# Expert stages of a four-layer network: second Gelu half also split into high and low f32r parts, its low part on GpSimd

## The chip, the cores and the metric

The kernel runs on one core of a Trainium2 chip. The metric is the device time of one execution in microseconds (us). The kernel before takes 1255.42 us, the median of 3 runs (1253.06 to 1261.09).

## The reference

The input x is [8, 512, 128] in float32. Four layers follow, each added to x: an RWKV-like time mixing, a mixture of experts, a causal attention with a phase term, and the same mixture of experts again. The change touches only the two expert layers. With the layer norm of x, written `tokens`, they compute:

```python
logits = tokens @ router_w.T
topv, topi = jax.lax.top_k(logits, K)              # K = 2 of E = 8 experts
w = jax.nn.softmax(topv, axis=-1)
gate = jnp.zeros((T, n_experts)).at[jnp.arange(T)[:, None], topi].add(w)
for e in range(n_experts):
    h = jax.nn.gelu(tokens @ w1[e].T, approximate=False)   # w1[e]: 256 x 128
    y = h @ w2[e].T                                        # w2[e]: 128 x 256
    out = out + gate[:, e:e + 1] * y
```

Every expert is computed for all tokens, and the gate (0 where an expert isn't chosen) weighs it.

## The kernel before

The program is a row of stages: time mixing (`rwkv_phase`), experts (`moe_phase`, tiles named moe_), attention, experts again (the same `moe_phase`), and the store. All instructions of a stage are written out engine by engine, and the order in each engine's stream is the order of the code. Engines meet only through semaphores.

In `moe_phase` the tokens are taken in 8 batches b of 512 tokens (T), channels on the 128 partitions. One step g = 8 b + e handles one expert e of one batch. The 256 hidden channels are two halves of 128 (k = 0, 1; HC = 2), so a step has

- `up(g)` on TensorE (L1774 on): for each half three matmuls in f32r into `ps_h`, weights high times x high, weights high times x low, weights low times x high (L1784 to L1786). A float32 value is split into a rounded high part and the rest, its low part; three f32r products stand for one float32 product.
- `gelu(g)` on ScalarE (L1859 on): of the first half a float32 Gelu into `hidden` (L1864) and the same Gelu rounded to f32r in `hidden_high` (L1865); of the second half the float32 Gelu alone (L1867). It waits for `down` of step g-2, because `hidden` has two places.
- `low_hidden(g)` on VectorE (L2012, L2017): `hidden_low` = `hidden` - `hidden_high` for the first half. Both inputs lie in SBUF.
- `down(g)` on TensorE (L1788 on): one float32 matmul for the second half (L1796, which the trace records as two instructions), then three f32r matmuls for the first half (L1800 to L1802), all into `ps_y`.
- `weigh(g)` on VectorE (L1986): `ps_y` (in PSUM) times the gate (in SBUF), and `accumulate(g)` (L1995): added to `total`, both inputs in SBUF. The first four steps of a stage are first copied out of PSUM by ScalarE (`keep_y`, L1878), and are weighed from SBUF.

TensorE's loop runs up(g+2), down(g). VectorE's loop runs in step g: low_hidden(g), weigh(g-1), accumulate(g-2), and then what is due. The table `WHEN` says in which step of which earlier batch the work that prepares batch c is done; for c of 4 and more: at e = 0 of batch c-2 the statistics of the norm (L199 to L208), at e = 1 the scaling (L218), at e = 2 the transposes on TensorE (`turn`, L1757), at e = 3 the copies (L1844, L1847) and the low part of x (L1925), at e = 4 the router (L1765), then five parts of the gates on VectorE at e = 5, 6, 7 and at e = 0, 1 of the next batch (L1934 to L1971), at e = 2 `fold` (L1770, waits for the last part of the gates). At e = 5 the output of the batch before is transposed (L1810), and at e = 6 added to x (`add`, L2000). So batches 1 to 5 carry statistics and scaling for a later batch in their steps 0 and 1, batch 0 carries two sets, and batches 6 and 7 none.

GpSimd has in this stage only eight small instructions, the power -0.5 of the variances (L224). It waits for the statistics, and the scaling waits for it.

At the start of the stage ScalarE rounds the up weights (w1) in four pieces and the down weights (w2), of the first halves only, in two (L1870, L1874); VectorE makes the low parts (L2005, L2010), some of them in the steps 0 and 1. `copies(0)` comes before them on ScalarE, and `gelu(0)`, `halve_gap(0)` (L1851, the tanh for which gates part 3 waits) behind.

## Time and profile before

| | |
|---|---|
| median of 3 runs | 1255.42 us |
| profiled execution, device time | 1258.44 us |
| its span, first to last instruction | 1256.7 us |
| TensorE busy | 1094.3 us (87%) |
| VectorE busy | 913.6 us (73%) |
| ScalarE busy | 658.0 us (52%) |
| GpSimd busy | 269.2 us (21%) |
| granted TensorE clock, mean | 0.918 of full |

The profile is one execution; busy times overlap between engines. The expert stages lie at about 300 to 523 us and 1025 to 1248 us of the span. A line's duration is from start to end of an instruction; where instructions of one engine follow without a gap, their starts are closer together than their durations, since the end of one overlaps the start of the next. "Idle before" is the time in which an engine had nothing, with what released it.

### The profile page before, as it was taken

The numbers are of one execution on the slowest core, as the hardware profiler recorded it, in microseconds if no ns is written. First come the engines' busy times: TensorE is split into PE (matmuls) and PEld (weight loads), VectorE is DVE, ScalarE is ACT, GpSimd is POOL, SyncE is SP. The second block draws the span as 40 slices with busy tenths as digits, with TensorE's granted clock in tenths as the row PEclk, the third lists the DMA queues.
The fourth block names the chain that finished last, engine by engine and source line by source line (L and its number), as shares of the span: only waits on it lengthen the run. The fifth ranks groups of instructions, "written<-read, shape, count | busy, mean of one in ns | idle before, by whom it ended". The sixth has DMA issues, their size and how long they took to land. (4 is left out here: it accounts for less than half of the span.)

```text
span 1256.7 us, 16161 instructions
## 1 busy us (share of the span) xinstructions
PE 1094.3 (87%) x5200; PEld 654.1 (52%) x5200; DVE 913.6 (73%) x1927; ACT 658.0 (52%) x1204; POOL 269.2 (21%) x300
## 2 busy tenths in 40 slices
PE   3888898975999999786888988989999969999996
PEld 1223333333666767444455555555656636767674
DVE  2778988993887776675766776767777628877775
ACT  1244434434555555388466665755755546555453
POOL 1455555650000000130122121222222210000000
PEclk9788888986999999888688988988989989999999
DMA  5000000000323322237977877778676212323221
GB/s 195 0 1 1 0 0 0 1 1 0 113 91 101 103 68 68 48 137 195 307 187 175 198 174 188 188 175 202 145 178 132 56 68 72 131 69 113 90 68 67
DMA packets 46478, 129.04 MB, mean 103 GB/s; under 512 B 6848, under 2 KB 8896, under 8 KB 39744
## 3 DMA queue, kind: packets, MB, share of 16 engines
q1 hardware_dynamic: 44352, 127.53, 37.1%
q8 instruction: 41, 0.67, 0.2%
q10 hardware_dynamic: 2048, 0.53, 0.2%
q14 instruction: 37, 0.30, 0.1%
HBM read 88.72 MB, written 36.70 MB: 100 GB/s over the span
## 5 line engine op out<-in xcount | busy, mean ns | idle before, releaser
L1483 DVE TENSOR_REDUCE attn_maxima<-attn_ps_p 128x1 f32<-128x512 f32 (+3 forms) x235 | 147.1, 638 | 81.3 <-PE attn_ps_p L987 56.8
L1864 ACT ACTIVATE moe_hidden<-moe_ps_h 128x512 f32<-128x512 f32 x128 | 76.3, 596 | 145.9 <-PE moe_ps_y L1802 144.1
L1402 POOL TENSOR_SCALAR_AFFINE_SELECT attn_probs<-attn_probs 128x512 f32<-128x512 f32 x128 | 83.8, 690 | 299.4 <-ACT attn_probs L1231 299.4
L982 PE MATMUL attn_ps_p<-attn_stack 96*128 96x384 f32 (+3 forms) x341 | 122.1, 401 | 7.8 <-DVE attn_maxima L1483 7.6
L1986 DVE TENSOR_TENSOR moe_gated<-moe_ps_y,moe_gate_all 128x512 f32<-128x512 f32 x106 | 73.2, 690 | 75.1 <-issue 46.7
L1030 PE MATMUL attn_ps_q<-attn_stack 128*128 128x128 f32 (+3 forms) x343 | 108.5, 380 | 18.2 <-DMA attn_stack<-attn_neg_max 14.5
L1784 PE MATMUL moe_ps_h<-moe_x_high,moe_w_high 128*128 128x512 f32 x256 | 107.3, 419 | 0.0
L1786 PE MATMUL moe_ps_h<-moe_x_high,moe_w_low 128*128 128x512 f32 x256 | 102.8, 402 | 0.0
L1785 PE MATMUL moe_ps_h<-moe_x_low,moe_w_high 128*128 128x512 f32 x256 | 102.3, 400 | 0.0
L1483 DVE TENSOR_REDUCE attn_maxima<-attn_ps_t 128x1 f32<-128x384 f32 (+3 forms) x117 | 74.6, 637 | 37.9 <-PE attn_ps_t L987 29.7
L1800 PE MATMUL moe_ps_y<-moe_hidden_high,moe_w_low 128*128 128x512 f32 x128 | 101.0, 789 | 0.0
L587 POOL TENSOR_TENSOR rwkv_rs<-rwkv_recept,rwkv_state 128x512 f32<-128x512 f32 x64 | 75.9, 1187 | 109.2 <-DVE rwkv_state L668 109.2
L668 DVE TENSOR_TENSOR_SCAN rwkv_state<-rwkv_decay,rwkv_kv 128x512 f32<-128x512 f32 x64 | 91.5, 1430 | 3.2
L2017 DVE TENSOR_TENSOR moe_hidden_low<-moe_hidden,moe_hidden_high 128x512 fp32r<-128x512 f32 x128 | 87.7, 685 | 6.2 <-ACT moe_hidden_high L1865 6.2
L1055 PE MATMUL attn_ps_o<-attn_probs,attn_v_ones 128*32 128x512 f32 (+3 forms) x1024 | 86.2, 456 | 1.7 <-POOL attn_probs L1402 1.7
L1030 PEld LDWEIGHTS attn_ps_q<-attn_stack 128*128 128x128 f32 x343 | 61.5, 202 | 42.3 <-DMA attn_stack<-attn_neg_max 16.9
L224 POOL TENSOR_TENSOR moe_rstd<-moe_var_eps,minus_half 128x4 f32<-128x4 f32 x16 | 16.1, 1008 | 311.4 <-DVE moe_var_eps L208 311.4
L982 PEld LDWEIGHTS attn_ps_p<-attn_stack 96*128 96x128 f32 x341 | 68.8, 215 | 20.3 <-DVE attn_maxima L1483 13.3
L1867 ACT ACTIVATE moe_hidden<-moe_ps_h 128x512 f32<-128x512 f32 x128 | 77.1, 602 | 0.4 <-PE moe_ps_h L1786 0.4
L1995 DVE TENSOR_TENSOR moe_total<-moe_total,moe_gated 128x512 f32<-128x512 f32 x112 | 76.4, 682 | 0.3
L1865 ACT ACTIVATE moe_hidden_high<-moe_ps_h 128x512 fp32r<-128x512 f32 x128 | 75.7, 591 | 0.0
L1228 ACT ACTIVATE attn_probs<-attn_ps_q 128x512 f32<-128x512 f32 x86 | 51.9, 603 | 36.6 <-PE attn_ps_q L1030 34.5
(256 smaller groups left out, 2441.5 us busy)
## 6 DMA issues: line engine op xcount, KB each, us to landing
moe_gate_all<-moe_gates SPq DMA_DIRECT2D x128, 256.0 KB, 4.8
attn_kept<-attn_parts SPq DMA_DIRECT2D x32, 768.0 KB, 4.7
attn_stack<-attn_kept SPq DMA_DIRECT2D x64, 384.0 KB
attn_stack<-attn_kept SPq DMA_DIRECT2D x64, 192.0 KB
attn_value<-attn_values SPq DMA_DIRECT2D x5, 1024.0 KB, 5.8
attn_value<-attn_values SPq DMA_DIRECT2D x5, 768.0 KB, 8.4
attn_values<-attn_early SPq DMA_DIRECT2D x2, 1792.0 KB, 5.7
attn_values<-attn_probs SPq DMA_DIRECT2D x2, 1792.0 KB, 21.7
```

What stands on the lines that cost most here:

```text
L668: nc.vector.tensor_tensor_scan(state[:, n, 1:T + 1], decay[:, s, :], kv[:, n % 2, :], 0.0, ALU.mult, ALU.add).then_inc(state_ready, 1)
L982: return mm(tiles(m)[:, i, :], stack[0][q][0:ROWS, h + i, t * P:(t + 1) * P], stack[1][q][0:ROWS, h + i, 0:(t + 1) * P], **flags)
L1030: return mm(ps_h[n % 3][:, at:at + width], stack[1][q][:, h, j * P:(j + 1) * P], stack[0][q][:, h, j * P:T], start=True, stop=True)
L1055: last = mm(ps_o[32 * hh:32 * hh + 32, j * P:T], v_ones[:, b % 2, j, 4 * g + hh, :], probs[:, g % 2, hh, at:at + width], start=(g % 2 == 0 ...
L1402: nc.gpsimd.affine_select(out=tile, in_=tile, compare_op=ALU.is_ge, fill=0.0, base=0, pattern=[[0, 4], [1, P]], channel_multiplier=-1).the ...
L1483: nc.vector.tensor_reduce(maxima[:, u % 2, h:h + heads, t], tiles, AX_X, ALU.max).then_inc(g_free, 1)
L1784: mm(out[:], w1_high[:, cols], x_high[:, c % 3, :], start=True, stop=False)
L1785: mm(out[:], w1_high[:, cols], x_low[:, c % 3, :], start=False, stop=False)
L1786: mm(out[:], w1_low[:, cols], x_high[:, c % 3, :], start=False, stop=True).then_inc(up_done, 1)
L1800: mm(ps_y[s][:], w2_low[:, first], hidden_high[:, s, :], start=False, stop=False)
L1867: fn(hidden[:, s, T:], ps_h[s][1][:], ACT.Gelu).then_inc(gelu_done, 1)
L2017: tt(hidden_low[:, s, :], hidden[:, s, 0:T], hidden_high[:, s, :].bitcast(F32), ALU.subtract).then_inc(low_ready, 1)
```

## The change

The second Gelu half is treated as the first. ScalarE computes it twice, in float32 and rounded to f32r (one more instruction a step, L1868 of the new file). Its low part is computed by GpSimd (`second_low`, L1911), which waits for the step's Gelu. `down` has six f32r matmuls in place of one float32 and three f32r; the first half comes first now, and its wait for `low_hidden` with it. The down weights are rounded and split for both halves, in four pieces of 512 columns in place of two, interleaved with the up weights. Nothing else changes; the order of the due work stays.

```diff
-        hidden_high = sb("hidden_high", [P, 2, T], F32R)
-        hidden_low = sb("hidden_low", [P, 2, T], F32R)
-        w2_high = sb("w2_high", [P, NE * C], F32R)
-        w2_low = sb("w2_low", [P, NE * C], F32R)
+        hidden_high = sb("hidden_high", [P, 2, HT], F32R)
+        hidden_low = sb("hidden_low", [P, 2, HT], F32R)
+        w2_high = sb("w2_high", [P, NE * HC * C], F32R)
+        w2_low = sb("w2_low", [P, NE * HC * C], F32R)
...
-        W1_STEP, W2_STEP = (1, 3, 4, 5), (2, 6)
+        W1_STEP, W2_STEP = (1, 3, 5, 7), (2, 4, 6, 8)
...
+                if g < NE and e % 2 == 0:
+                    pe.wait_ge(split, W2_STEP[e // 2])
+                pe.wait_ge(low_ready, g + 1)
+                mm(ps_y[s][:], w2_low[:, first], hidden_high[:, s, 0:T], start=True, stop=False)
+                mm(ps_y[s][:], w2_high[:, first], hidden_high[:, s, 0:T], start=False, stop=False)
+                mm(ps_y[s][:], w2_high[:, first], hidden_low[:, s, 0:T], start=False, stop=False)
                 pe.wait_ge(gelu_done, g * HC + 2)
-                mm(ps_y[s][:], w2_cols[:, second], hidden[:, s, T:], start=True, stop=False)
-                pe.wait_ge(low_ready, g + 1)
-                if g in (0, NE // 2):
-                    pe.wait_ge(split, W2_STEP[g // (NE // 2)])
-                mm(ps_y[s][:], w2_low[:, first], hidden_high[:, s, :], start=False, stop=False)
-                mm(ps_y[s][:], w2_high[:, first], hidden_high[:, s, :], start=False, stop=False)
-                mm(ps_y[s][:], w2_high[:, first], hidden_low[:, s, :], start=False, stop=True).then_inc(down_done, 1)
+                mm(ps_y[s][:], w2_low[:, second], hidden_high[:, s, T:], start=False, stop=False)
+                mm(ps_y[s][:], w2_high[:, second], hidden_high[:, s, T:], start=False, stop=False)
+                pe.wait_ge(second_low_ready, g + 1)
+                mm(ps_y[s][:], w2_high[:, second], hidden_low[:, s, T:], start=False, stop=True).then_inc(down_done, 1)
...
-                fn(hidden[:, s, T:], ps_h[s][1][:], ACT.Gelu).then_inc(gelu_done, 1)
+                fn(hidden[:, s, T:], ps_h[s][1][:], ACT.Gelu)
+                fn(hidden_high[:, s, T:], ps_h[s][1][:], ACT.Gelu).then_inc(gelu_done, 1)
...
+            def second_low(g):
+                s = g % 2
+                pool.wait_ge(gelu_done, (g + 1) * HC)
+                if g >= 2:
+                    pool.wait_ge(down_done, g - 1)
+                nc.gpsimd.tensor_tensor(hidden_low[:, s, T:], hidden[:, s, T:], hidden_high[:, s, T:].bitcast(F32),
+                                        ALU.subtract).then_inc(second_low_ready, 1)
+
             norm.on_pool(pool, 0)
             for b in range(NB):
                 for e in range(NE):
+                    second_low(b * NE + e)
                     for c in due("stats", b, e):
                         norm.on_pool(pool, c)
...
                     low_hidden(g)
-                    if g == 0:
-                        split_w1(2)
-                    if g == 1:
-                        split_w1(3)
-                        split_w2(1)
+                    if g < 3:
+                        split_w2(g + 1)
+                    if g < 2:
+                        split_w1(g + 2)
```

On TensorE, in step 0 of the first batch, from the last matmul of an `up` on, the stream before has one float32 matmul (L1796) and three f32r ones after `fold`:

```order
L1786 MATMUL moe_ps_h<-moe_x_high,moe_w_low 128x512
L1770 MATMUL moe_ps_r<-identity,moe_gate 32x128
L1796 MATMUL moe_ps_y<-moe_hidden,experts_in_w 128x512
L1800 MATMUL moe_ps_y<-moe_hidden_high,moe_w_low 128x512
L1801 MATMUL moe_ps_y<-moe_hidden_high,moe_w_high 128x512
L1802 MATMUL moe_ps_y<-moe_hidden_low,moe_w_high 128x512
```

and of the change, at the same place:

```order
L1783 MATMUL moe_ps_h<-moe_x_high,moe_w_low 128x512
L1767 MATMUL moe_ps_r<-identity,moe_gate 32x128
L1795 MATMUL moe_ps_y<-moe_hidden_high,moe_w_low 128x512
L1796 MATMUL moe_ps_y<-moe_hidden_high,moe_w_high 128x512
L1797 MATMUL moe_ps_y<-moe_hidden_low,moe_w_high 128x512
L1799 MATMUL moe_ps_y<-moe_hidden_high,moe_w_low 128x512
L1800 MATMUL moe_ps_y<-moe_hidden_high,moe_w_high 128x512
L1802 MATMUL moe_ps_y<-moe_hidden_low,moe_w_high 128x512
```

The float32 matmul has gone, three f32r matmuls of the second half stand behind those of the first; `hidden_low` of the first half is read by the third.

On GpSimd, in the first expert stage, the difference of the two streams is this (a minus is before, a plus is the change):

```order
-L224 TENSOR_TENSOR moe_rstd<-moe_var_eps,minus_half 128x4 x8
+L1904 UNCONDITIONAL_BRANCH
+L224 TENSOR_TENSOR moe_rstd<-moe_var_eps,minus_half 128x4
+L1911 TENSOR_TENSOR moe_hidden_low<-moe_hidden,moe_hidden_high 128x512
+L224 TENSOR_TENSOR moe_rstd<-moe_var_eps,minus_half 128x4
+L1911 TENSOR_TENSOR moe_hidden_low<-moe_hidden,moe_hidden_high 128x512
+L224 TENSOR_TENSOR moe_rstd<-moe_var_eps,minus_half 128x4
+L1911 TENSOR_TENSOR moe_hidden_low<-moe_hidden,moe_hidden_high 128x512 x7
+L224 TENSOR_TENSOR moe_rstd<-moe_var_eps,minus_half 128x4
+L1911 TENSOR_TENSOR moe_hidden_low<-moe_hidden,moe_hidden_high 128x512 x8
```

The small powers were alone; now 64 subtractions of 128x512 stand between them, one a step, and the power of a statistics step stands behind that step's own subtraction and ahead of the next one's.

On ScalarE, at the start of the first expert stage, before, from the rounding of x on:

```order
L1847 CAST moe_x_high<-moe_ps_t 128x512
L1870 CAST moe_w_high<-experts_in_w 128x512
L1874 CAST moe_w_high<-experts_in_w 128x512
L1870 CAST moe_w_high<-experts_in_w 128x512 x3
L1874 CAST moe_w_high<-experts_in_w 128x512
L1864 ACTIVATE moe_hidden<-moe_ps_h 128x512
L1865 ACTIVATE moe_hidden_high<-moe_ps_h 128x512
L1867 ACTIVATE moe_hidden<-moe_ps_h 128x512
L1851 ACTIVATE moe_tanh_gap<-moe_gap_of_two 128x4
```

and of the change, from the fifth rounding of weights on:

```order
L1871 CAST moe_w_high<-experts_in_w 128x512
L1874 CAST moe_w_high<-experts_in_w 128x512
L1871 CAST moe_w_high<-experts_in_w 128x512
L1874 CAST moe_w_high<-experts_in_w 128x512
L1864 ACTIVATE moe_hidden<-moe_ps_h 128x512
L1865 ACTIVATE moe_hidden_high<-moe_ps_h 128x512
L1867 ACTIVATE moe_hidden<-moe_ps_h 128x512
L1868 ACTIVATE moe_hidden_high<-moe_ps_h 128x512
L1851 ACTIVATE moe_tanh_gap<-moe_gap_of_two 128x4
```

There are eight roundings where there were six, and four Gelus where there were three, ahead of the tanh.

## Rows read from the trace of the kernel before

**Rows 1.** Busy time by engine in both expert stages, and in steps 1-7 of batch 0

```profile
core 0: us, PE busy (x) PEld busy (x) DVE busy (x) ACT busy (x) POOL busy (x), PEclk, DMA share, GB/s
300.00:523.50 223.50, 210.04 (x840) 148.15 (x840) 169.91 (x462) 117.40 (x235) 8.07 (x8) 0.97 0.24 77
1025.00:1256.70 231.70, 209.94 (x840) 148.09 (x840) 170.20 (x463) 117.61 (x235) 8.07 (x8) 0.96 0.27 92
317.60:340.60 23.00, 22.89 (x98) 16.59 (x98) 20.03 (x58) 15.13 (x32) 1.01 (x1) 1.00 0.28 93
```

**Rows 2.** Timeline of TensorE and ScalarE, one quiet step (start, duration, ... [idle before])

```profile
506.51 0.40 PE L1784 MATMUL moe_ps_h<-moe_x_high,moe_w_high 128*128 128x512 f32 x1
506.71 0.60 ACT L1864 ACTIVATE moe_hidden<-moe_ps_h 128x512 f32<-128x512 f32 x1 [1.37 <-PE moe_ps_y L1802]
...
507.21 0.59 ACT L1865 ACTIVATE moe_hidden_high<-moe_ps_h 128x512 fp32r<-128x512 f32 x1
...
507.69 0.60 ACT L1867 ACTIVATE moe_hidden<-moe_ps_h 128x512 f32<-128x512 f32 x1
...
507.92 1.02 PE L1796 MATMUL moe_ps_y<-moe_hidden,experts_in_w 128*128 128x512 f32 x2
...
509.00 0.39 PE L1801 MATMUL moe_ps_y<-moe_hidden_high,moe_w_high 128*128 128x512 f32 x1
...
509.23 0.40 PE L1802 MATMUL moe_ps_y<-moe_hidden_low,moe_w_high 128*128 128x512 f32 x1
...
509.46 0.39 PE L1784 MATMUL moe_ps_h<-moe_x_high,moe_w_high 128*128 128x512 f32 x1
```

**Rows 3.** Durations by line (min/median/max ns), GpSimd and VectorE, time mixing and expert stage

```profile
L587 POOL TENSOR_TENSOR rwkv_rs<-rwkv_recept,rwkv_state x64: 1087/1259/1452, 42.0 to 281.4; 128x512 f32<-128x512 f32 x64
L203 DVE TENSOR_TENSOR rwkv_sums<-rwkv_stats x8: 171/946/1054, 10.9 to 220.7; 128x12 f32<-128x12 f32 x8
L203 DVE TENSOR_TENSOR moe_sums<-moe_stats x16: 171/172/173, 300.7 to 1175.9; 128x12 f32<-128x12 f32 x16
L651 DVE SCALAR_TENSOR_TENSOR rwkv_z<-rwkv_z,rwkv_gate x8: 665/1516/1610, 100.1 to 296.0; 128x512 f32<-128x512 f32 x8
L662 DVE TENSOR_TENSOR rwkv_kv<-rwkv_key,rwkv_ps_v x64: 654/677/689, 40.0 to 279.2; 128x512 f32<-128x512 f32 x64
```

**Rows 4.** Timeline of GpSimd and VectorE in the time mixing

```profile
91.94 1.08 POOL L581 TENSOR_TENSOR rwkv_xf<-rwkv_mixed,rwkv_xT 128x512 f32<-128x512 f32 x1
92.00 1.05 DVE L203 TENSOR_TENSOR rwkv_sums<-rwkv_stats 128x12 f32<-128x12 f32 x1
```

**Rows 5.** Timeline of VectorE and GpSimd, step 6 of batch 2 to step 2 of batch 3

```profile
388.85 0.69 DVE L1986 TENSOR_TENSOR moe_gated<-moe_ps_y,moe_gate_all 128x512 f32<-128x512 f32 x1 [0.95 <-PE moe_ps_y L1802]
...
390.61 0.68 DVE L2000 TENSOR_TENSOR x_rows<-x_rows,moe_ps_t 128x512 f32<-128x512 f32 x1
391.20 0.68 DVE L2017 TENSOR_TENSOR moe_hidden_low<-moe_hidden,moe_hidden_high 128x512 fp32r<-128x512 f32 x1
...
393.63 0.68 DVE L2017 TENSOR_TENSOR moe_hidden_low<-moe_hidden,moe_hidden_high 128x512 fp32r<-128x512 f32 x1
...
394.75 0.69 DVE L1986 TENSOR_TENSOR moe_gated<-moe_ps_y,moe_gate_all 128x512 f32<-128x512 f32 x1 [0.44 <-issue]
...
397.73 1.01 POOL L224 TENSOR_TENSOR moe_rstd<-moe_var_eps,minus_half 128x4 f32<-128x4 f32 x1 [25.33 <-DVE moe_var_eps L208]
...
398.03 0.68 DVE L2017 TENSOR_TENSOR moe_hidden_low<-moe_hidden,moe_hidden_high 128x512 fp32r<-128x512 f32 x1
...
399.83 1.11 DVE L218 TENSOR_SCALAR moe_xn<-x_rows,moe_mean,moe_rstd 128x128 f32<-128x128 f32 x4
...
401.00 0.66 PE L1757 MATMUL moe_ps_t<-identity,moe_xn 128*128 128x128 f32 x4 [0.44 <-DVE moe_xn L218]
...
401.41 0.21 DVE L1971 TENSOR_TENSOR moe_gate<-moe_first,moe_second 128x32 f32<-128x32 f32 x1
```

**Rows 6.** Timeline of the start of the first expert stage

```profile
308.55 0.62 ACT L1874 CAST moe_w_high<-experts_in_w 128x512 fp32r<-128x512 f32 x1
...
309.58 0.60 ACT L1864 ACTIVATE moe_hidden<-moe_ps_h 128x512 f32<-128x512 f32 x1 [0.40 <-PE moe_ps_h L1786]
...
311.58 0.17 DVE L1960 TENSOR_SCALAR moe_share<-moe_tanh_gap 128x4 f32<-128x4 f32 x1 [0.50 <-ACT moe_tanh_gap L1851]
...
317.71 0.66 PE L1757 MATMUL moe_ps_t<-identity,moe_xn 128*128 128x128 f32 x4 [1.69 <-DVE moe_xn L218]
```

**Rows 7.** Timeline of the end of the first expert stage

```profile
516.01 0.60 ACT L1864 ACTIVATE moe_hidden<-moe_ps_h 128x512 f32<-128x512 f32 x1 [1.81 <-PE moe_ps_y L1802]
...
517.87 0.68 DVE L2017 TENSOR_TENSOR moe_hidden_low<-moe_hidden,moe_hidden_high 128x512 fp32r<-128x512 f32 x1
...
519.18 0.40 PE L1802 MATMUL moe_ps_y<-moe_hidden_low,moe_w_high 128*128 128x512 f32 x1
```

28 lines of the change are left out of this document (11 added, 17 removed).

## The prediction

> **What bounds the kernel now.** I first read the busy time of the two expert stages, the only code touched: TensorE is busy 210.04 of 223.5 us and 209.94 of 231.7, VectorE 170, ScalarE 117, GpSimd 8 [rows 1]. So TensorE paces them. Then one quiet step in the timelines [rows 2]. From the first matmul of one `up` (506.51) to that of the next (509.46) a step takes 2.95 us with no gap: `up` 1.41 (six f32r matmuls of 0.235), `down` 1.54. In `down` an f32r matmul costs 0.23 from start to start (509.00, 509.23, 509.46), so the float32 one costs 1.54 - 3 x 0.23 = 0.85. ScalarE idles 1.37 us ahead of its three Gelus, so a fourth seems free. Last, the places where TensorE doesn't pace. In steps 0 and 1 of batches 1 to 5 VectorE has statistics, gates and scaling on top of its share; there the transposes at 401.00 come after 0.44 us of idle, "until" the scaling, and from the `weigh` at 394.75 to the last gate operation (start 401.41) VectorE has no idle time [rows 5]. At the start of the stage the transposes wait 1.69 us for the scaling [rows 6].
>
> **Removed and added, on TensorE.** Each of 128 steps trades 0.85 for 3 x 0.233 = 0.70: 0.15 saved, 19.2 us in all if nothing else changed. A quiet step falls to 2.80. The Trainium skill, "TensorE: Matmul & The Clock Gate", section "Wait — 56ns, not 53.3ns?", gives 215.7 ns from start to start for 512 columns at full clock. An estimate by it would be 0.85 - 0.65 = 0.20 a step, so 6.4 us more gained; the trace shows 0.23, at a granted clock of 1.00, and decides.
>
> **Added on ScalarE.** One more Gelu, 0.48 from start to start. Four end 2.05 us after the first starts (0.50 + 0.48 + 0.48 + 0.59 [rows 2]); with idle 1.37 in a step of 2.95, that leaves about 0.74 in one of 2.80. I cost it at nothing; without that cover it would be 0.48 a step. Only the start of the stage pays, below.
>
> **Added on GpSimd, and what it does to VectorE.** 128 subtractions of 128x512. The nearest row is its own multiply of that shape, 1.09 us at least, median 1.26 [rows 3]. I take 1.05 to 1.1. It fits in GpSimd's idle time. But the trace of the time mixing shows what happens beside it. VectorE's L203, twelve elements wide, takes 0.17 us in the expert stages, yet up to 1.05 and 0.95 in the median in the time mixing [rows 3]; in the timeline it starts at 92.00 and lasts 1.05 while GpSimd's L581 runs from 91.94 for 1.08 [rows 4]. L651, both inputs in SBUF, has a median of 1.52 against 0.67 at best; L662, one input in PSUM, never passes 0.69 in 64 executions [rows 3]. So a VectorE instruction with two SBUF inputs waits until GpSimd's ends, and one that reads PSUM doesn't. In the expert stages nothing met GpSimd so far. Now `low_hidden`, `accumulate`, most of the gates and the small statistics can meet it; `weigh`, `add`, the low part of x don't.
>
> In a quiet step the subtraction fits: it runs from 2.1 to 3.2 us after the Gelu's release, `weigh` starts at 2.8 and the `accumulate` behind it at 3.4. Where VectorE is behind, it doesn't. I walk a statistics batch from the `weigh` at 388.85 (call it 0) [rows 5]:
>
> Before: `add` at 1.76, `low_hidden` of step 7 at 2.35, that of the next step 0 at 4.78, `weigh` at 5.90 after 0.44 idle, `low_hidden` of step 1 at 9.18, scaling at 10.98, gates done 12.8. `fold` on TensorE waits for those.
>
> After: step 7's Gelus start with the `weigh`, so its subtraction runs 2.05 to 3.15; `low_hidden` waits 0.8, until 3.15. `weigh`, `accumulate` (0.6 each) to 4.95. The next subtraction takes over at 4.95, until 6.0: the gates part 2 wait 1.05. They take 0.6, `low_hidden` of step 0 ends at 7.2; TensorE would have reached its `down` at 6.8, starts at 7.25. `weigh`, `accumulate` to 8.4, statistics 1.6 to 10.0, gates part 3 to 10.5, `low_hidden` to 11.1, where TensorE wanted it at 10.05. GpSimd's power runs 10.05 to 11.05 and the subtraction behind it 11.1 to 12.15: `weigh` passes, `accumulate` waits 0.45 and ends at 12.75, scaling 13.8, gates 14.5. That is 1.7 us later than before. The four steps left until the next such `weigh` are paced by TensorE: -0.6. **Sum +1.1 a batch, five batches: +5.5 a stage.**
>
> **Batch 0.** Before the first Gelu there are two more roundings, 0.52 each, of which 0.40 was idle, and the start goes from 309.58 to 310.1; the fourth Gelu puts the tanh, and gates part 3, from 311.58 to 312.35 [rows 6]. The first subtraction then holds gates part 4 until 313.3, one more split costs 0.6 ahead of the statistics, and the transposes go from 317.71 to 319.6: +1.9. Up to 340.6 VectorE gets two more splits (1.2) and five waits for GpSimd that a walk like the one above gives (1.0, 0.85, 0.6, 0.85, 0.45); it had 23.00 - 20.03 = 2.97 us idle there [rows 1]. 1.9 + 4.95 - 2.97 = **+3.9**.
>
> **Batches 6 and 7 and the end.** Batch 6 has no statistics: 8 x -0.15, and 0.85 of the same two early waits: -0.35. Batch 7: -1.2. At the end the last Gelus start at 516.01, done 518.06; `low_hidden`, from 517.87, holds GpSimd until 518.55, its subtraction ends at 519.6, and the last matmul starts then, in place of 519.18 [rows 7]: with the last step's saving lost, +0.5.
>
> **Sum.** 3.9 + 5.5 - 0.35 - 1.2 + 0.5 = 8.35 a stage, 16.7 for both. The second stage I take as the first. From the profiled execution's 1258.4 that is 1275.1; it stands 3.0 above the median of the runs shown, so for the median I forecast 1255.4 + 16.7 = 1272.
>
> **The rivals.**
>
> *No such waits matter, and the kernel gets faster.* GpSimd and VectorE may meet less than in my walk, since each meeting hangs on a few tenths (the first: subtraction from 2.05, `low_hidden` at 2.35). With no meeting, a statistics batch gains the 0.44 idle's part and its quiet steps, 2 x 0.15 + 4 x 0.15 = 0.9; a stage is then -0.1 (batch 0: extra splits and tanh +1.1, steps -1.2), -4.5, -2.4, +0.3: -6.7, twice -13.4, 1242. It speaks for it that ScalarE and GpSimd have room; against it that in batch 0 and around steps 7, 0, 1 VectorE goes without a break, so a subtraction must push something. It decides when a batch's waits on its unbroken chain come to less than about 0.6 us in place of 2.3. Chance 0.2.
>
> *Half of the waits.* Some fall under `weigh`, `add` or the statistics' first part. With 1.2 us of waits a batch in place of 2.3, stages come out near 0: 1250 to 1266. Chance 0.25.
>
> *The walk holds.* Own range 1266 to 1280, chance 0.43.
>
> *The scaling is held too.* L218 reads one SBUF tensor and writes SBUF. No row shows it beside a big GpSimd instruction. If it is held as well, scaling beside a subtraction loses up to 1.05 us in each of seven preparations a stage: 14.7 us for both, 1272 + 15 = 1287. The Trainium skill, "SBUF — State Buffer", section "Who interferes with whom", says that a tensor_scalar can enter a mode that takes both read ports, and then whoever issues second blocks fully; by that rule L218 belongs here. Chance 0.12.
>
> **How the numbers follow.** About 1% is what a measurement of this kernel can tell from no change: 1243 and 1268 are its edges. Faster: the first rival about at its edge and a little more, 0.17. Slower: most of the walk (0.38), the held scaling (0.12) and a small part of the half case (0.05): 0.55. Between: 0.28. The range reaches from the upper part of the first rival, 1245, to the held scaling, 1288; what is left out is about 0.1 on each side.
>
> **What would show it.** TensorE: a quiet step of 2.80, and six matmuls in `down` at 0.23. VectorE: `low_hidden` and `accumulate` with maxima near 1.7 where they had 0.69, L1986 unchanged; idle time of TensorE ahead of the first matmul of `down`, released by `low_hidden`, in steps 0 and 1, and ahead of the transposes above 1 us. If L218 stays at 0.34, the last rival is out. If `low_hidden` and `accumulate` keep 0.68, my theory is wrong, and so it is if GpSimd's subtraction takes 2 us: then TensorE waits for GpSimd itself. If the saving is not 0.15 a step, that term is wrong.

## The result, and the profile after

The changed kernel takes 1303.17 us (median of 4 runs, 1302.65 to 1303.64); the kernel before takes 1258.26 us beside it (1253.06 to 1262.67). The ratio is 1.0354, with an interval of 1.0321 to 1.0387: slower, and by 45 us where 17 were forecast. The time lies above the forecast range of 1245 to 1288.

The page of the profile after, span and busy times:

```profile
span 1301.0 us, 16803 instructions
PE 1093.1 (84%) x5328; PEld 684.8 (53%) x5328; DVE 972.3 (75%) x1931; ACT 721.4 (55%) x1336; POOL 444.2 (34%) x428
```

The two expert stages, as in [rows 1] (same columns: TensorE, weight loads, VectorE, ScalarE, GpSimd, granted clock):

```profile
294.60:540.40 245.80, 210.68 (x904) 162.71 (x904) 199.51 (x464) 148.97 (x301) 95.89 (x72) 0.94 0.21 70
1043.20:1301.00 257.80, 213.36 (x904) 165.29 (x904) 199.47 (x464) 149.09 (x301) 96.66 (x72) 0.92 0.24 83
```

In the first stage TensorE is still busy 210.68 us, as before (210.04), but the stage takes 245.8 us instead of 223.5, so TensorE is not busy for 35 us of it instead of 13. VectorE's busy time rose from 169.9 to 199.5 us with as many instructions (464 and 462): some of them take longer. GpSimd works 96 us where it worked 8.

From the first transposes of the stage to the start of attention, the first stage grew from 219.8 us to 242.0 (303.84 to 523.64, now 298.49 to 540.45). From its first transposes to the store, the second grew from 220.5 (1029.44 to 1249.96) to 247.2 (1047.14 to 1294.38). That is 48.9 us more in the stages, 22.2 in the first and 26.7 in the second, of which 4.6 came back in code that wasn't touched: the time mixing ends 5.4 earlier, attention takes 0.9 more, the end 0.1 less. In the time mixing TensorE was granted 0.90 of its full clock in the first 290 us where it was 0.88 in the execution before; I read that as a difference between executions.

**The quiet step** came out as forecast. Timeline of TensorE and ScalarE, to compare with [rows 2]:

```profile
503.06 0.60 ACT L1864 ACTIVATE moe_hidden<-moe_ps_h 128x512 f32<-128x512 f32 x1 [0.72 <-PE moe_ps_y L1802]
...
504.27 0.40 PE L1795 MATMUL moe_ps_y<-moe_hidden_high,moe_w_low 128*128 128x512 f32 x1
504.51 0.40 PE L1796 MATMUL moe_ps_y<-moe_hidden_high,moe_w_high 128*128 128x512 f32 x1
...
505.21 1.29 POOL L1911 TENSOR_TENSOR moe_hidden_low<-moe_hidden,moe_hidden_high 128x512 fp32r<-128x512 f32 x1 [1.49 <-ACT moe_hidden_high L1868]
505.43 0.39 PE L1802 MATMUL moe_ps_y<-moe_hidden_low,moe_w_high 128*128 128x512 f32 x1
...
505.86 0.60 ACT L1864 ACTIVATE moe_hidden<-moe_ps_h 128x512 f32<-128x512 f32 x1 [0.73 <-PE moe_ps_y L1802]
```

From Gelu to Gelu it is 2.80 us (503.06 to 505.86), matmuls in `down` start every 0.23, and ScalarE idles 0.72 (0.74 forecast). Each part of TensorE's gain is there. The last matmul at 505.43 starts when the subtraction of 505.21 has just begun; the one it reads is that of the step before, 502.42 to 503.72.

**The rest** of a batch is not. Timeline of VectorE, GpSimd, one Gelu and the waits of TensorE, from step 7 of batch 2 to step 2 of batch 3, to compare with [rows 5]:

```profile
396.78 1.29 POOL L1911 TENSOR_TENSOR moe_hidden_low<-moe_hidden,moe_hidden_high 128x512 fp32r<-128x512 f32 x1 [1.72 <-ACT moe_hidden_high L1868]
397.05 1.57 DVE L2024 TENSOR_TENSOR moe_hidden_low<-moe_hidden,moe_hidden_high 128x512 fp32r<-128x512 f32 x1
...
399.58 1.39 POOL L1911 TENSOR_TENSOR moe_hidden_low<-moe_hidden,moe_hidden_high 128x512 fp32r<-128x512 f32 x1 [1.51 <-ACT moe_hidden_high L1868]
399.75 1.28 DVE L1955 SCALAR_TENSOR_TENSOR moe_rest<-moe_first,moe_logits 128x32 f32<-128x32 f32 x1
...
405.03 1.01 POOL L224 TENSOR_TENSOR moe_rstd<-moe_var_eps,minus_half 128x4 f32<-128x4 f32 x1 [4.06 <-DVE moe_var_eps L208]
...
405.40 0.62 ACT L1868 ACTIVATE moe_hidden_high<-moe_ps_h 128x512 fp32r<-128x512 f32 x1
...
406.01 2.95 POOL L1911 TENSOR_TENSOR moe_hidden_low<-moe_hidden,moe_hidden_high 128x512 fp32r<-128x512 f32 x2
...
406.16 0.47 PE L1795 MATMUL moe_ps_y<-moe_hidden_high,moe_w_low 128*128 128x512 f32 x1 [0.84 <-DVE moe_hidden_low L2024]
406.53 1.31 DVE L2002 TENSOR_TENSOR moe_total<-moe_total,moe_gated 128x512 f32<-128x512 f32 x1
...
407.76 2.05 DVE L218 TENSOR_SCALAR moe_xn<-x_rows,moe_mean,moe_rstd 128x128 f32<-128x128 f32 x4
...
409.87 0.66 PE L1754 MATMUL moe_ps_t<-identity,moe_xn 128*128 128x128 f32 x4 [2.02 <-DVE moe_xn L218]
```

Call it a meeting when a VectorE instruction runs beside one of GpSimd and lasts longer for it. The three meetings of the walk are there: `low_hidden` 1.57 instead of 0.68, the first operation of the gates part 2 1.28 instead of 0.19, `accumulate` 1.31 instead of 0.68. There is a fourth: the row of GpSimd at 406.01 holds two subtractions, the one of step 1 and right behind it the one of step 2. Step 1's had to wait behind the power (405.03, until 406.04), and by then step 2's Gelus were done too (405.40, until 406.02). Beside the second subtraction the four scalings take 2.05 instead of 1.11. Of the 14 preparations behind the first of each stage, 11 have a scaling of 2.04 to 2.06; the other three keep 1.1. The transposes then come after 2.02 us of idle instead of 0.44. Starts of the transposes in the first stage were 348.49, 374.82, 401.00, 427.34, 453.70 before, a period of 26.2 to 26.4; now they are 350.79, 379.73, 409.87, 438.61, 468.80, so a batch takes 28.7 to 28.9 or 30.1 to 30.2.

Durations by line over the whole execution (min/median/max ns), for [rows 3]:

```profile
L1911 POOL TENSOR_TENSOR moe_hidden_low<-moe_hidden,moe_hidden_high x128: 1260/1296/1857, 306.9 to 1288.4; 128x512 fp32r<-128x512 f32 x128
L2024 DVE TENSOR_TENSOR moe_hidden_low<-moe_hidden,moe_hidden_high x128: 676/684/1576, 309.0 to 1288.2; 128x512 fp32r<-128x512 f32 x128
L2002 DVE TENSOR_TENSOR moe_total<-moe_total,moe_gated x112: 672/681/1681, 328.8 to 1292.0; 128x512 f32<-128x512 f32 x112
L1993 DVE TENSOR_TENSOR moe_gated<-moe_ps_y,moe_gate_all x106: 673/691/694, 333.2 to 1291.3; 128x512 f32<-128x512 f32 x106
L218 DVE TENSOR_SCALAR moe_xn<-x_rows,moe_mean,moe_rstd x64: 331/335/1290, 297.3 to 1222.8; 128x128 f32<-128x128 f32 x64
```

Medians hide it: of these lines the maxima of `low_hidden`, `accumulate` and the scaling moved and the medians didn't. `weigh`, which reads PSUM, kept 694.

**The clock.** In two-microsecond windows behind three of the waits, with one at full clock for comparison (390 to 392; same columns as rows 1; the granted clock is the third number from the end):

```profile
380.00:382.00 2.00, 2.00 (x10) 1.35 (x9) 2.00 (x4) 1.08 (x2) 1.22 (x1) 0.78 0.00 0
382.00:384.00 2.00, 2.00 (x6) 1.61 (x6) 1.63 (x6) 0.00 (x0) 0.00 (x0) 0.50 0.00 0
...
390.00:392.00 2.00, 2.00 (x12) 1.64 (x12) 0.53 (x1) 0.59 (x2) 1.17 (x1) 1.00 0.90 279
...
440.00:442.00 2.00, 2.00 (x6) 1.56 (x5) 1.11 (x2) 2.00 (x5) 0.01 (x1) 0.50 0.07 16
...
470.00:472.00 2.00, 2.00 (x6) 1.51 (x6) 1.29 (x2) 2.00 (x6) 0.00 (x0) 0.50 0.05 12
```

Behind the waits at 379.73, 438.61 and 468.80 TensorE is granted 0.50 for two to four microseconds, the lower of its levels (1.2 instead of 2.4 GHz), and two microseconds hold 6 of its matmuls instead of 12. Behind the waits at 350.79 and 409.87 it isn't. In both stages, behind batch 0, 7 of 10 such waits are followed by a fall. The periods that contain a fall take 30.1 to 31.1 us, those that don't 28.7 to 28.9. Before, there was no such fall between 313 and 523 us. In batch 0 the change's clock also falls behind the wait of 4.25 us (0.57 at 316 to 318).

### The profile page after: what moved, and what is told of

It reads as the page before. It is cut to its first block and busy times, and to the rows that moved or that the text cites. A ratio compares the mean times of both kernels' runs of the same rounds, so it can differ in the third digit from the quotient of the medians.

```text
span 1301.0 us, 16803 instructions
## 1 busy us (share of the span) xinstructions
PE 1093.1 (84%) x5328; PEld 684.8 (53%) x5328; DVE 972.3 (75%) x1931; ACT 721.4 (55%) x1336; POOL 444.2 (34%) x428
## 5 line engine op out<-in xcount | busy, mean ns | idle before, releaser
L1911 POOL TENSOR_TENSOR moe_hidden_low<-moe_hidden,moe_hidden_high 128x512 fp32r<-128x512 f32 x128 | 176.9, 1384 | 241.0 <-ACT moe_hidden_high L1868 241.0
L1781 PE MATMUL moe_ps_h<-moe_x_high,moe_w_high 128*128 128x512 f32 x256 | 110.4, 431 | 0.0
L1783 PE MATMUL moe_ps_h<-moe_x_high,moe_w_low 128*128 128x512 f32 x256 | 106.5, 416 | 0.0
L1782 PE MATMUL moe_ps_h<-moe_x_low,moe_w_high 128*128 128x512 f32 x256 | 106.1, 415 | 0.0
L2024 DVE TENSOR_TENSOR moe_hidden_low<-moe_hidden,moe_hidden_high 128x512 fp32r<-128x512 f32 x128 | 96.4, 753 | 4.8 <-ACT moe_hidden_high L1865 4.6
L2002 DVE TENSOR_TENSOR moe_total<-moe_total,moe_gated 128x512 f32<-128x512 f32 x112 | 88.0, 786 | 0.3
L1868 ACT ACTIVATE moe_hidden_high<-moe_ps_h 128x512 fp32r<-128x512 f32 x128 | 78.9, 617 | 0.0
L1865 ACT ACTIVATE moe_hidden_high<-moe_ps_h 128x512 fp32r<-128x512 f32 x128 | 75.9, 593 | 0.0
```

Of the source, the lines that this page charges most:

```text
L1781: mm(out[:], w1_high[:, cols], x_high[:, c % 3, :], start=True, stop=False)
L1782: mm(out[:], w1_high[:, cols], x_low[:, c % 3, :], start=False, stop=False)
L1783: mm(out[:], w1_low[:, cols], x_high[:, c % 3, :], start=False, stop=True).then_inc(up_done, 1)
L1911: nc.gpsimd.tensor_tensor(hidden_low[:, s, T:], hidden[:, s, T:], hidden_high[:, s, T:].bitcast(F32), ALU.subtract).then_inc(second_low_re ...
L2002: tt(total[:, b % 2, :], total[:, b % 2, :], gated[:, g % 3, :], ALU.add).then_inc(summed, 1)
L2024: tt(hidden_low[:, s, 0:T], hidden[:, s, 0:T], hidden_high[:, s, 0:T].bitcast(F32), ALU.subtract).then_inc(low_ready, 1)
```

## The experiments

Eleven kernels ran. Each was timed beside the kernel before on the same chip; that one had medians of 1257.31, 1258.00 and 1256.08 us in the three groups (x1 to x4; x5, x7 to x9; x10, x12, x13). Period and idle time are those of the fourth to the last transposes of the first stage. The last column adds up the two stages in the one profiled execution, each from its first transposes, to the start of attention and to the store; it leaves out the code that no kernel changes, in which the executions differ by several us (attention takes 501.5 to 511.7 us in these traces).

| kernel | median us | ratio to before (95%) | period of a batch, first stage | idle ahead of the transposes | both stages, us |
|---|---|---|---|---|---|
| before | 1256.08 to 1258.26 | 1 | 26.2 to 26.4 | 0.44 to 1.21 | 440.3 |
| changed | 1303.17 | 1.0354 (1.0321 to 1.0387) | 28.7 to 30.2 | 1.96 to 2.29 | 489.2 |
| x1 GpSimd only writes | 1246.09 | 0.9888 (0.9825 to 0.9951) | 25.2 to 25.5 | 0.54 to 1.17 | 436.0 |
| x2 half of the columns | 1261.15 | 1.0035 (1.0007 to 1.0062) | 26.4 to 26.6 | 0.92 to 1.15 | 446.7 |
| x3 before, plus a subtraction | 1310.73 | 1.0383 (1.0320 to 1.0445) | 30.6 to 31.0 | 1.66 to 3.09 | 497.7 |
| x4 filler matmuls | 1296.81 | 1.0313 (1.0253 to 1.0373) | 28.8 to 29.0 | 0.32 to 0.64 | 478.3 |
| x5 low part on VectorE | 1266.11 | 1.0063 (1.0034 to 1.0091) | 27.0 to 27.1 | 1.10 to 1.24 | 449.4 |
| x7 subtraction in steps 3 to 6 | 1258.60 | 1.0003 (0.9973 to 1.0032) | 25.2 to 25.4, first 27.2 | 0.51 to 1.54 | 446.1 |
| x8 in steps 7, 0, 1, 2 | 1289.58 | 1.0268 (1.0235 to 1.0300) | 27.0, then 28.5 to 30.3 | 1.75 to 2.02 | 476.5 |
| x10 all but step 2 | 1280.52 | 1.0169 (1.0130 to 1.0208) | 27.6 to 27.8, first 29.3 | 1.01 to 2.04 | 465.7 |
| x12 batch 0 only | 1256.44 | 0.9999 (0.9972 to 1.0026) | 25.2 to 25.5 | 0.52 to 1.54 | 445.8 |
| x9 mixed, steps 3 to 6 | 1249.98 | 0.9947 (0.9918 to 0.9976) | 25.5 to 25.7, first 26.3 | 0.44 to 0.60 | 431.6 |
| x13 mixed, steps 2 to 6 | 1256.19 | 1.0005 (0.9979 to 1.0031) | 26.3 to 26.5, first 27.3 | 0.34 to 1.55 | 439.5 |

**x1_write_only.** Is it the reading by GpSimd, or the extra work on TensorE and ScalarE?

```diff
-                nc.gpsimd.tensor_tensor(hidden_low[:, s, T:], hidden[:, s, T:], hidden_high[:, s, T:].bitcast(F32),
-                                        ALU.subtract).then_inc(second_low_ready, 1)
+                nc.gpsimd.memset(hidden_low[:, s, T:].bitcast(F32), 0.0).then_inc(second_low_ready, 1)
```

> The changed kernel, but GpSimd writes zeros into the low part of the second half (a memset of 128x512) in place of the subtraction, so the low part of the second half is left out; everything else (four Gelus, six f32r matmuls, four pieces of down weights, the wait for GpSimd) stays. Theory (a GpSimd instruction that reads SBUF holds up VectorE instructions with two SBUF inputs and the scaling, and the long waits let TensorE's clock fall): the holds go, the saving of 0.15 us a step stays, about 1245 us, VectorE lines back at 0.68. Rival one (what costs is the fourth Gelu, the extra splits or the new order in down): stays at about 1300. Rival two (any GpSimd instruction on SBUF holds VectorE, writing ones too): VectorE's two-input lines still reach over 1 us, 1265 to 1280.

It took 1246.09 us. Durations by line:

```profile
L1911 POOL MEMSET moe_hidden_low<- x128: 524/525/644, 308.8 to 1236.8; 128x512 f32 x128
L2023 DVE TENSOR_TENSOR moe_hidden_low<-moe_hidden,moe_hidden_high x128: 679/683/693, 310.1 to 1236.6; 128x512 fp32r<-128x512 f32 x128
L218 DVE TENSOR_SCALAR moe_xn<-x_rows,moe_mean,moe_rstd x64: 334/343/628, 299.3 to 1175.1; 128x128 f32<-128x128 f32 x64
```

So all of the change but the subtraction gains about 12 us by the medians, close to the 13.4 that the prediction gave for no meetings. In the trace the two stages gain only 4.3 (436.0 against 440.3): the periods are shorter by 0.9, but up to the fourth transposes the stages take 2.9 and 5.1 us more than before. The rest of the 12 lies in other code or in the spread of the four runs (1239 to 1251, the profiled one at 1251). A GpSimd instruction that only writes doesn't hold `low_hidden` (693 at most, though dozens of `low_hidden` and `accumulate` overlap a MEMSET). It does hold the scaling, up to 628.

**x2_half_columns.** Does the cost follow the length of the subtraction?

```diff
-                nc.gpsimd.tensor_tensor(hidden_low[:, s, T:], hidden[:, s, T:], hidden_high[:, s, T:].bitcast(F32),
-                                        ALU.subtract).then_inc(second_low_ready, 1)
+                half = T + T // 2
+                nc.gpsimd.tensor_tensor(hidden_low[:, s, T:half], hidden[:, s, T:half],
+                                        hidden_high[:, s, T:half].bitcast(F32), ALU.subtract).then_inc(second_low_ready, 1)
```

> The changed kernel, but GpSimd subtracts only 256 of the 512 columns (half of the low part of the second half isn't made, and the last matmul of down takes the first half's low part in its place). Theory: each hold shrinks from 1.3 us to about 0.75, the transposes wait less than 1.5 us, and the clock no longer falls in the middle of a stage: a batch with statistics takes 26.5 to 27.5 us in place of 28.7 to 30.2, about 1270 us in all. Rival (GpSimd's cost is the latency or the number of its instructions, not how long each holds the port): 1295 to 1303.

It took 1261.15 us. A subtraction of 256 columns takes 0.74 in the median in place of 1.30, `low_hidden` is at most 1.02 and the scaling at most 0.76. The period is 26.4 to 26.6, where 28.7 to 30.2 and 25.4 stand at both ends. Half the length costs a good quarter of the whole (1246 to 1261 of 1246 to 1303), less than the 1270 that I had put. The maxima show that each meeting is shorter; that there are also fewer of them is my reading.

**x3_before_plus_sub.** The kernel before with the subtraction alone, whose result nobody reads, and for which the last matmul of `down` waits:

```diff
+                pe.wait_ge(extra_done, g + 1)
...
+                nc.gpsimd.tensor_tensor(unused[:, s, :], hidden[:, s, T:], hidden_high[:, s, :].bitcast(F32),
+                                        ALU.subtract).then_inc(extra_done, 1)
```

> The kernel before, with one thing added: a GpSimd subtraction of 128x512 from hidden and hidden_high into a tile that nobody reads, once a step, with TensorE's last matmul of down waiting for it as in the change. TensorE, ScalarE and the splits are as before. Theory: the holds alone cost nearly the whole loss and the missing saving of 19 us comes on top of it only partly: VectorE's chain in steps 6 to 1 is as long as in the change, a batch with statistics takes 28.5 to 30 us, 1290 to 1305 us in all. Rival (the loss is in the rest of the change): 1258 to 1265.

It took 1310.73 us, 5.7 us above the expected range; that the order of TensorE's old `down` fits worse with the subtraction is my reading, which no run takes apart. Timeline in the first stage:

```profile
407.42 2.95 POOL L1915 TENSOR_TENSOR moe_unused<-moe_hidden,moe_hidden_high 128x512 fp32r<-128x512 f32 x2
...
408.75 0.49 PE L1804 MATMUL moe_ps_y<-moe_hidden_low,moe_w_high 128*128 128x512 f32 x1 [0.54 <-POOL moe_unused L1915]
409.17 2.05 DVE L218 TENSOR_SCALAR moe_xn<-x_rows,moe_mean,moe_rstd 128x128 f32<-128x128 f32 x4
...
411.27 0.76 PE L1758 MATMUL moe_ps_t<-identity,moe_xn 128*128 128x128 f32 x4 [2.02 <-DVE moe_xn L218]
```

Without any of the other parts the same pair of subtractions stands beside the same scaling, and the same wait of 2.02 follows. TensorE itself waits for GpSimd here, 0.54 in this place. x1 and x3 together show that the subtraction on GpSimd is the cause.

**x4_filler.** What does the clock cost? Fourteen short matmuls into the bank of the transposes stand ahead of each wait for the scaling, from the transposes of batch 1 on. They are extra work whose results the transposes overwrite.

```diff
-                pe.wait_ge(norm.normed, c + 1)
...
+                if c >= 1:
+                    for _ in range(14):
+                        mm(ps_t[:, 0:256], w1_high[:, 0:P], x_high[:, (c - 1) % 3, 0:256], start=True, stop=True)
+                pe.wait_ge(norm.normed, c + 1)
```

> The changed kernel, with 14 matmuls of 256 columns that nobody needs on TensorE ahead of each wait of the transposes for the scaling (from batch 1's on), written where the transposes write later. Theory that the falls of TensorE's clock to half are part of the loss, some 1.4 us each: they go in the middle of the stages, batches that took 30.1 us take 28.7, about 8 to 12 us less in all, 1291 to 1296. Rival (the clock isn't on the path, VectorE is, since the steps behind the transposes have slack): 1301 to 1305, or more where the filler itself is late.

It took 1296.81 us, 0.8 above its range. Windows at the place of a fall, and in batch 0:

```profile
382.00:384.00 2.00, 2.00 (x9) 1.60 (x10) 1.92 (x7) 0.23 (x2) 0.00 (x0) 1.00 0.00 0
...
316.00:318.00 2.00, 2.00 (x7) 1.62 (x6) 1.93 (x11) 2.00 (x5) 0.00 (x0) 0.59 0.83 218
```

From the fourth transposes on, the clock stays at full and each period is 28.8 to 29.0, with none of 30.1; in batch 0, where 2.60 us of idle are left, it still falls. That shows that the later falls come from the waits and make the difference between 28.8 and 30.1. By the medians they cost 6 us; the intervals of the two ratios (1.0313 and 1.0354) overlap, so the times alone don't fix the size. In the traces the two stages take 10.9 us less than those of the change, of which up to 1.6 is another wait, for the gates' transfer (see the next section).

**x5_on_vector.** The second low part on VectorE, right behind `low_hidden`; GpSimd doesn't subtract.

```diff
+            def second_low(g):
+                s = g % 2
+                v.wait_ge(gelu_done, (g + 1) * HC)
+                tt(hidden_low[:, s, T:], hidden[:, s, T:], hidden_high[:, s, T:].bitcast(F32),
+                   ALU.subtract).then_inc(second_low_ready, 1)
```

> The changed kernel with the second low part made by VectorE, right behind low_hidden of the same step; GpSimd has only its eight small powers a stage again, all else as changed. Theory (the meetings of a 1.3 us GpSimd instruction with VectorE are what costs): an operation of VectorE costs it 0.6 us from start to start, a meeting up to 1.3. Steps 7, 0 and 1 of a statistics batch get 3 x 0.6 = 1.8 us more on the unbroken chain, the four paced steps give 0.6 back: period 26.3 + 1.2 = 27.5, batch 0 two us more, end nothing: about 8 us a stage, 1258 + 16 = 1274, range 1262 to 1288. L218 stays at 0.34 and low_hidden at 0.68. Rival (it is the work itself, and not who does it or what it meets): like the change, 1297 to 1303, or more, since VectorE is the busier engine.

It took 1266.11 us, with 27.0 to 27.1 a batch (27.5 expected) and the scaling at 0.348 at most. The engine that was already late does all of the extra work, and the kernel is 37 us faster than with the work on the idle engine. So the place on an idle engine was worth less than nothing: a subtraction costs VectorE 0.6 us when it does it, and up to 1.1 more in one instruction (1.28 for 0.19) when GpSimd does.

**x7_quiet_steps and x8_busy_steps.** Where do the meetings cost? x7 subtracts in steps 3 to 6 of each batch and writes zeros in the others, x8 the reverse.

```diff
-                nc.gpsimd.tensor_tensor(hidden_low[:, s, T:], hidden[:, s, T:], hidden_high[:, s, T:].bitcast(F32),
-                                        ALU.subtract).then_inc(second_low_ready, 1)
+                if 3 <= g % NE <= 6:
+                    nc.gpsimd.tensor_tensor(hidden_low[:, s, T:], hidden[:, s, T:],
+                                            hidden_high[:, s, T:].bitcast(F32), ALU.subtract).then_inc(second_low_ready, 1)
+                else:
+                    nc.gpsimd.memset(hidden_low[:, s, T:].bitcast(F32), 0.0).then_inc(second_low_ready, 1)
```

> The changed kernel, in which GpSimd makes the low part of the second half only in steps 3 to 6 of each batch; in steps 0, 1, 2 and 7 it writes zeros to it (a memset of 0.52 us), so that the low part of the second half is left out of the result there. If the cost lies where VectorE has no slack (steps 7, 0, 1, 2), this one comes near the writing alone (1246): 1246 to 1253, turns every 25.2 to 25.6 us with idle under 1.2, clock at full. Rival, that each subtraction costs something wherever it stands: about half way between 1246 and 1303, 1270 to 1280.

> The other half: GpSimd subtracts only in steps 7, 0, 1 and 2, and writes zeros in steps 3 to 6, so that the low part of the second half is left out of the result there. If the cost lies in the steps without slack, it is the change's own: 1292 to 1303, turns every 28.5 us or more with idle of about 2 us, and the clock falls behind these waits. Rival, cost spread evenly: 1270 to 1280.

x8 took 1289.58 us, 2.4 below its range, but much nearer to the change than to the rival's 1270 to 1280, with turns after 2.02 us of idle and the clock at 0.50 at 402 to 404 and at 0.57 around 434. x7 took 1258.60 us, 5.6 above its range. Its turns (transposes), in the timeline of the first stage:

```profile
400.19 1.11 DVE L218 TENSOR_SCALAR moe_xn<-x_rows,moe_mean,moe_rstd 128x128 f32<-128x128 f32 x4
...
401.36 0.66 PE L1754 MATMUL moe_ps_t<-identity,moe_xn 128*128 128x128 f32 x4 [0.51 <-DVE moe_xn L218]
```

From the fifth transposes of the stage on (376.14) its periods are 25.2 to 25.4, the same as with no subtraction at all (x1): in the quiet steps it is free there. Of the 12.5 us that it takes more than x1, 9.9 lie ahead of that: from the first transposes to the fifth it takes 77.5 us in the first stage and 82.9 in the second, x1 takes 73.0 and 77.5. My division was too coarse: in batch 0, with two sets of statistics, the splits and the early steps weighed from SBUF, no step is quiet, and the turn behind it (27.2) is late as well.

**x12_batch_zero.** The subtraction in batch 0 alone, zeros behind.

```diff
-                if 3 <= g % NE <= 6:
+                if g < NE:
```

(the minus line is that of x7).

> The changed kernel with the subtraction in batch 0 alone and writes of zeros in batches 1 to 7 (the low part of the second half is left out of the result there). It prices the meetings of batch 0. From the starts of the transposes, the change takes 4.8 and 5.5 us more than the writing alone (1246) up to the first turn behind batch 0: 1246 + 10 = 1256, range 1252 to 1259, with periods of 25.2 to 25.4 behind. Rival, that batch 0 costs the 3.9 a stage of the prediction less the extra roundings and splits, which the writing alone has too (about 1 to 2): 1248 to 1250.

It took 1256.44 us, as expected: meetings in batch 0 cost 10 us in both stages by the medians, 14 by the ratios (0.9999 against 0.9888, each uncertain by 3 to 8 us). In the traces the two stages take 9.8 us more than x1's, and no more than x7's (445.8 and 446.1), which subtracts only in steps 3 to 6 of this batch. The start of the first stage shows two meetings of batch 0, one with a small TENSOR_SCALAR, for which no row of before shows a meeting. Timeline of the changed kernel, for [rows 6]:

```profile
306.90 1.29 POOL L1911 TENSOR_TENSOR moe_hidden_low<-moe_hidden,moe_hidden_high 128x512 fp32r<-128x512 f32 x1 [9.61 <-ACT moe_hidden_high L1868]
306.95 1.27 DVE L1967 TENSOR_SCALAR moe_share<-moe_tanh_gap 128x4 f32<-128x4 f32 x1 [1.22 <-ACT moe_tanh_gap L1851]
...
313.54 1.26 POOL L1911 TENSOR_TENSOR moe_hidden_low<-moe_hidden,moe_hidden_high 128x512 fp32r<-128x512 f32 x1
313.61 2.04 DVE L218 TENSOR_SCALAR moe_xn<-x_rows,moe_mean,moe_rstd 128x128 f32<-128x128 f32 x4 [1.12 <-POOL moe_rstd L224]
...
315.70 0.55 PE L1754 MATMUL moe_ps_t<-identity,moe_xn 128*128 128x128 f32 x3 [4.25 <-DVE moe_xn L218]
```

A TENSOR_SCALAR of four elements with one SBUF input takes 1.27 in place of 0.17, and the scaling is held here too; TensorE waits 4.25 where it waited 1.69.

**x10_not_step_two.** Is the fourth meeting, that of the scaling, caused by step 2's subtraction, and what is it worth? Zeros are written in step 2 alone.

```diff
-                if 3 <= g % NE <= 6:
+                if g % NE != 2:
```

(the minus line is again that of x7).

> The changed kernel, in which GpSimd writes zeros in place of the subtraction in step 2 of each batch alone (the low part of the second half is left out of the result there). In the trace of the change the last of the subtractions that stand beside the scaling L218 is that of step 2. If it holds the scaling and nothing else: L218 back to about 0.34, the turn's wait from 2.0 to about 1.1, the period from 28.8 to 27.9, and the clock stays full, since waits of 1.1 us did not bring it down in the kernel with the work on VectorE: 1303 - 9 - 6 = 1288, range 1282 to 1294. Rival, that the scaling would be late anyhow because of the meetings ahead of it: 1297 to 1303.

It took 1280.52 us, 1.5 us below the range. Timeline in the first stage:

```profile
406.93 1.29 POOL L1912 TENSOR_TENSOR moe_hidden_low<-moe_hidden,moe_hidden_high 128x512 fp32r<-128x512 f32 x1
...
407.46 1.31 DVE L2005 TENSOR_TENSOR moe_total<-moe_total,moe_gated 128x512 f32<-128x512 f32 x1
408.16 0.53 POOL L1915 MEMSET moe_hidden_low<- 128x512 f32 x1
...
408.69 1.10 DVE L218 TENSOR_SCALAR moe_xn<-x_rows,moe_mean,moe_rstd 128x128 f32<-128x128 f32 x4
...
409.86 0.66 PE L1754 MATMUL moe_ps_t<-identity,moe_xn 128*128 128x128 f32 x4 [1.08 <-DVE moe_xn L218]
```

`accumulate` is still held (1.31), the scaling is back at 1.10, the wait is 1.08, and behind batch 0 the clock fell only once in the stage, after the one wait of 2.04 at 352.92. The steady period of 27.6 to 27.8 is the walk of the prediction, which gave 26.3 + 1.1 = 27.4. In batch 0 nothing changed (the transposes still wait 4.26 us): there it is the subtraction of step 1 that stands beside the scaling.

**x9_hybrid.** Can the gain be had without the meetings? It starts from the kernel before and takes the new step only where VectorE has slack and no more due work of batch 0 lies; the down weights of the second halves are rounded and split in steps 4 to 6 of batch 1. ScalarE's fourth Gelu and GpSimd's subtraction go with these steps.

```diff
+        SPLIT = [g for g in range(2 * NE, NB * NE - 1) if 3 <= g % NE <= 6 or g >= 6 * NE + 2]
...
+                if g in SPLIT:
...
+                    mm(ps_y[s][:], w2_low[:, first], hidden_high[:, s, 0:T], start=True, stop=False)
+                    mm(ps_y[s][:], w2_high[:, first], hidden_high[:, s, 0:T], start=False, stop=False)
+                    mm(ps_y[s][:], w2_high[:, first], hidden_low[:, s, 0:T], start=False, stop=False)
+                    pe.wait_ge(gelu_done, g * HC + 2)
+                    mm(ps_y[s][:], second_w2_low[:, first], hidden_high[:, s, T:], start=False, stop=False)
+                    mm(ps_y[s][:], second_w2_high[:, first], hidden_high[:, s, T:], start=False, stop=False)
+                    pe.wait_ge(second_low_ready, SPLIT.index(g) + 1)
+                    mm(ps_y[s][:], second_w2_high[:, first], hidden_low[:, s, T:], start=False, stop=True).then_inc(down_done, 1)
+                    return
```

> The kernel before, with the new step (six f32r matmuls, four Gelus, subtraction on GpSimd) only in steps 3 to 6 of batches 2 to 5 and in the steps from step 2 of batch 6 on but the last: 29 steps a stage. Nothing is left out. If the saving of 0.15 us a step is real and the subtraction is free where VectorE has slack: 2 x 29 x 0.15 = 8.7 us less, about 1249, ratio 0.993. If the subtraction costs wherever it stands, or the extra roundings and VectorE's split of the down weights in steps 4 to 6 of batch 1 are not hidden: 1256 to 1262, ratio 1.000 to 1.004.

It took 1249.98 us, the forecast 1249: faster than before by 0.5% (0.2 to 0.8%), and than the change by 4%. The two stages take 8.7 us less in its trace (431.6 against 440.3), and 8.7 were expected. The scaling keeps 0.347 at most, and TensorE waits as before:

```profile
393.61 1.11 DVE L218 TENSOR_SCALAR moe_xn<-x_rows,moe_mean,moe_rstd 128x128 f32<-128x128 f32 x4
...
394.78 0.65 PE L1762 MATMUL moe_ps_t<-identity,moe_xn 128*128 128x128 f32 x4 [0.44 <-DVE moe_xn L218]
```

**x13_hybrid_five.** One step more, step 2 of batches 2 to 5, is 0.15 us less work for TensorE each time, and puts a subtraction beside the scaling.

```diff
-        SPLIT = [g for g in range(2 * NE, NB * NE - 1) if 3 <= g % NE <= 6 or g >= 6 * NE + 2]
+        SPLIT = [g for g in range(2 * NE, NB * NE - 1) if 2 <= g % NE <= 6 or g >= 6 * NE + 2]
```

> The mixed kernel (1250, new step in steps 3 to 6) with the new step in step 2 of batches 2 to 5 as well. Nothing is left out. TensorE saves 0.15 a step more, 1.2 us in all; but GpSimd's subtraction of step 2 now stands beside the scaling. If that holds the scaling (up to 1 us in each of eight batches): period 26.3 to 26.5 in place of 25.6, the turn's wait 1.3 in place of 0.44, total 1250 - 1 + 8 = 1257, ratio 0.999 to 1.002. Rival, that it passes beside it: 1249, ratio 0.993.

It took 1256.19 us (1257 expected), and the whole gain is gone:

```profile
395.50 1.27 POOL L1935 TENSOR_TENSOR moe_hidden_low<-moe_hidden,moe_hidden_high 128x512 fp32r<-128x512 f32 x1 [1.05 <-ACT moe_hidden_high L1887]
395.55 2.08 DVE L218 TENSOR_SCALAR moe_xn<-x_rows,moe_mean,moe_rstd 128x128 f32<-128x128 f32 x4
...
397.69 0.66 PE L1762 MATMUL moe_ps_t<-identity,moe_xn 128*128 128x128 f32 x4 [1.41 <-DVE moe_xn L218]
```

Here the scaling's meeting stands by itself, with none ahead of it: 0.97 us on VectorE (2.08 against 1.11), 0.97 on TensorE's wait (1.41 against 0.44), 0.8 in the period, eight times; the two stages take 7.9 us more than x9's.

## Why the prediction was wrong

The direction was right (slower, chance 0.55), the size wrong: 45 us where the sum gave 17. The runs make a chain from before to the change (us). The ratios are taken times 1258, and each of their steps is uncertain by 6 to 9, as the intervals of its two ratios say; the stages are one profiled execution each.

| step | forecast | both stages, traces | by the ratios |
|---|---|---|---|
| before to x1, no subtraction | -13.4 | -4.3 | -14 |
| to x12, meetings of batch 0 | +8.0 | +9.8 | +14 |
| to x10, meetings of steps 7, 0 and 1 and the ends | +22.1 | +19.9 | +21 |
| to x4, scaling held | 0 | +12.6 | +18 |
| to the change, falls of the clock | 0 | +10.9 | +5 |
| sum | +16.7 | +48.9 | +44 |

So three terms are missing from the sum: the held scaling, the clock and, by the traces, 9 us that are lost even without a subtraction, most of them in batch 0.

- **TensorE's saving of 0.15 a step, the fourth Gelu for nothing:** right. The quiet step is 2.80, ScalarE idles 0.72 for 0.74, and x9 shows the gain of its 58 steps in the stages (8.7 forecast and measured). The 13.4 without meetings is met by x1's median and ratio (12 to 14), but not by its stages (4.3): that agreement is at least in part luck.
- **Which VectorE instructions are held:** right for those with two SBUF inputs, and `weigh` is free of it, as said.
- **Length of the subtraction:** I took 1.05 to 1.1 near the fastest row of [rows 3] (1087) and not its median (1259). It takes 1.26 at least and 1.296 in the median. The three meetings cost 0.89, 1.09 and 0.63 instead of 0.8, 1.05 and 0.45: 0.3 a batch, 3 us in all.
- **The walk of a batch, +1.1:** the order of its three meetings was right, and x10's 27.7 is 0.3 above its 27.4. From x12 to x10 the terms of the walk without batch 0 give 22 (ten times 1.1 + 0.9, 1.7 for the batches 6, 0.4 for the ends); 21 was measured by the ratios, 19.9 in the stages.
- **The step that failed: "scaling 13.8" in the walk.** I ended GpSimd's work at 12.15 with the subtraction of step 1 and let the scaling run from 12.75. I left out the subtraction of step 2, whose Gelus were done by then: GpSimd goes from one to the next (406.01, x2, 2.95). So a subtraction did stand beside the scaling. Whether it holds one was the other half, and I gave it 0.12 because "no row shows it". It does: 14 preparations by 1.05 were worked out as 14.7; from x10 to x4 it is 12.6 in the stages and 18, uncertain by 9, by the ratios. The trace of the change shows 11 of the 14 held, by 0.94 each (2.05 for 1.11), so the size was about right and the chance was not. The Trainium skill, "SBUF — State Buffer", section "Who interferes with whom", says that a tensor_scalar may take both of VectorE's ports and is then exclusive with GpSimd. The trace agrees, for the scaling (1290 against 335) and for four elements (1.27 us). By the same section an instruction with two SBUF inputs passes beside one that only writes; x1 agrees (693), and its scaling, held by the writing (628), agrees with the first sentence. Without a row either way, and with that page for it, this was at least an even chance; it should have been in the sum or the range's middle.
- **The clock was missing,** a second step that failed: it stood at nothing in the sum without a reason. No step of mine asked what longer waits do to the granted clock. Behind batch 0, 7 of the change's 10 waits of 1.96 us and more are followed by 0.50, those of 1.0 to 1.2 us in x5 and in x10 never. It needed the scaling's microsecond on top: the walk alone gave waits of 1.08, with the clock at full. By the medians it cost 6 us, by the stages up to 10.9; a period with a fall is 30.1 against 28.8.
- **Batch 0, +3.9 a stage:** too small. From the first to the fourth transposes the change takes 7.7 us more than before in the first stage and 10.6 in the second. The start was right: the first Gelu comes 0.53 later (0.52 put) and the tanh 0.72 (0.77 put), counted from the first transposes. The meetings were mis-sized by little: 4.0 and 5.8 in the traces (x12 less x1), 5 to 7 by the times, where 4.0 was in the sum. Most is in what the sum without meetings put at -0.1: up to the fourth transposes x1, without any subtraction, takes 2.9 and 5.1 more than before. I left out that the scaling is held here too, beside the subtraction of step 1 (313.54): the transposes wait 4.25 and start 17.21 after the first ones (13.87 before), +3.3 where I gave +1.9; in x1 it is 15.43.
- **Its idle time as cover, and the second stage "as the first":** the second stage grew by 26.7, the first by 22.2. One thing differs that I hadn't read. In step 1 of batch 1 VectorE waits for the gates' transfer:

```profile
1099.88 0.69 DVE L1993 TENSOR_TENSOR moe_total<-moe_ps_y,moe_gate_all 128x512 f32<-128x512 f32 x1 [2.98 <-DMA moe_gate_all<-moe_gates]
```

In the kernel before the same wait in the second stage was 0.62:

```profile
1072.51 0.69 DVE L1986 TENSOR_TENSOR moe_total<-moe_ps_y,moe_gate_all 128x512 f32<-128x512 f32 x1 [0.62 <-DMA moe_gate_all<-moe_gates]
```

It doesn't follow the subtractions: in the second stage it is 3.92 in x1, which has none, 1.42 in x4 and 0.89 in x10, which have all or nearly all, 1.01 in x9, and x5 shows no such wait. So it is no part of the meetings, but it blurs the stages by up to 3 us: 3.3 of x1's 5.1 in batch 0 are this wait. What sets it stays open; each kernel was profiled once.
- **The rival "no such waits", 0.2**, came near x1's median (1242 against 1246) but not its stages, and was wrong that it could occur: in steps 7, 0 and 1 the meetings hit an unbroken chain. **"Half of the waits"** fell with it.

## What to carry to other kernels

Work moved to an idle GpSimd is not free when VectorE has no slack: ask of every VectorE instruction beside it whether it has two SBUF inputs or is a TENSOR_SCALAR from SBUF to SBUF, and walk all of GpSimd's instructions, to the last one that may be released by then. Put such work into the steps in which the other engine has slack, and leave the rest as it was. Where a wait of TensorE grows by a microsecond at a place that recurs, count what the clock loses behind it as well.

## What the runs showed of the hardware

- A GpSimd subtraction of 128x512 from SBUF with an f32r output takes 1.26 us at least, 1.296 in the median and up to 1.86 beside VectorE's work; a MEMSET of the same tile takes 0.525 in the median. With 256 columns the subtraction takes 0.74.
- A VectorE instruction that is held lasts until about the end of GpSimd's, small ones too: 128x32 takes 1.28 us (0.19 before), 128x4 1.27 (0.17 before). One that reads PSUM isn't held: `weigh`, of which dozens overlap a subtraction, takes 694 ns at most.
- A TENSOR_SCALAR from SBUF to SBUF is held by reading and by only writing GpSimd instructions (1290 and 628 against 335 ns), a TENSOR_TENSOR with two SBUF inputs only by the former (1576 and 693 against 684).
- TensorE's granted clock fell to 0.50 of full behind idle times of about 2.0 us in the stage, but not behind each of them (379.73 and 438.61 yes, 409.87 and 350.79 no), and behind batch 0 it stayed at full when short matmuls filled part of the wait.
